# SyncE's order of issue inside an attention slot: the shift ahead of the stacks, and a finished group's rows and denominators loaded in two slots

## The reference

```python
x = queries
q = relu(layernorm(x) @ Wq.T + bq); k = relu(keys @ Wk.T + bk); v = relu(values @ Wv.T + bv)
score = einsum('bhsd,bhtd->bhst', qh, kh) / sqrt(8)
a = einsum('bhst,bhtd->bhsd', softmax(score), vh)
a = transpose(a, (0, 1, 3, 2)).reshape(...)            # per head, feature before token
x = x + layernorm(a + layernorm(x))
x = x + layernorm(ffn(layernorm(x)))                   # self-attention, experts, two layer norms
```

## Time and profile before

| | |
|---|---|
| median of 3 runs | 668.88 us (664.58 to 671.4) |
| the profiled execution | 670.79 us, of which the span of the core is 669.0 us |
| busy in the span | PE 532.2, PEld 212.6, DVE 539.4, ACT 429.6, POOL 229.0 us |
| cross-attention, slots 0 to 31 | from about 70 to 403 us of the span |
| the rest of the program (self-attention, experts) | from 403 us to the end |
| chain that ended last | PE 38%, DVE 27%, POOL 15%, ACT 8%, issue 8%, DMA 3% |

### The profile page before, as it was taken

How to read it: one execution, slowest core, us unless ns; L and a number is a source line. 1 busy time by engine, 2 the same in 40 slices (tenths; PEclk the granted TensorE clock), 3 DMA queues, 4 the chain that set the end, 5 groups by cost and what they waited for, 6 DMA issues and landing times.

```text
span 669.0 us, 9878 instructions
## 1 busy us (share of the span) xinstructions
PE 532.2 (80%) x3439; PEld 212.6 (32%) x3439; DVE 539.4 (81%) x867; ACT 429.6 (64%) x914; POOL 229.0 (34%) x360
## 2 busy tenths in 40 slices
PE   2884799999999998999999988476587685998710
PEld 1550122222222222222222215355467542443300
DVE  4969699999999998999999800988838156899996
ACT  2550489998898888988889885134344404566554
POOL 7001000000034440354403650662344401676761
PEclk9995599999999999999999999688687775999955
DMA  9832010111111111201221002000000000000112
GB/s 243 255 136 106 14 37 23 40 33 46 54 60 30 34 53 47 65 26 32 59 57 49 8 9 62 15 1 1 0 1 1 1 1 0 0 1 0 32 31 63
DMA packets 31285, 28.92 MB, mean 43 GB/s; under 512 B 6132, under 2 KB 23676, under 8 KB 31236
## 3 DMA queue, kind: packets, MB, share of 16 engines
q1 hardware_dynamic: 29204, 27.31, 13.8%
q10 hardware_dynamic: 2032, 0.98, 0.6%
HBM read 19.23 MB, written 8.65 MB: 42 GB/s over the span
## 4 chain that ended last, share of the span: by engine, by line
PE 38%; DVE 27%; POOL 15%; ACT 8%; issue 8%; DMA 3%; SPq 1%; ACTq 0%; DVEq 0%; POOLq 0%
PE ps L1267 11%; PE ps L1262 8%; DVE row_max L1436 8%; PE ps L1235 4%; PE ps L593 3%; DVE space L872 2%; DVE st L241 2%; POOL space L382 2%; POOL space L384 2%; POOL smallp L379 2%; ACT attended L1384 1%; DMA space<-max_turned 1%; PE ps L578 1%; DVE space L863 1%; DVE space L264 1%
## 5 line engine op out<-in xcount | busy, mean ns | idle before, releaser
L1436 DVE TENSOR_REDUCE row_max<-ps 128x2 f32<-128x1024 f32 x256 | 299.7, 1219 | 20.2 <-PE ps L1235 17.3
L1368 ACT ACTIVATE space<-ps 128x512 f32<-128x512 f32 x512 | 271.9, 605 | 45.0 <-PE ps L1262 44.5
L1262 PE MATMUL ps<-space 51*128 51x512 bf16 x512 | 159.5, 388 | 9.6 <-DMA space<-max_turned 5.8
L1267 PE MATMUL ps<-space 128*32 128x512 f32 x1024 | 138.1, 612 | 3.0 <-ACT space L1368 0.7
L1235 PE MATMUL ps<-space 48*128 48x512 bf16 x512 | 128.8, 401 | 14.2 <-DVE row_max L1436 12.5
L1137 POOL CAST max_parts<-row_max 128x16 bf16<-128x16 f32 x32 | 6.3, 197 | 269.9 <-DVE row_max L1436 269.9
L1262 PEld LDWEIGHTS ps<-space 51*128 51x128 bf16 x512 | 41.2, 94 | 170.9 <-ACT space L1368 149.1
L593 PE MATMUL ps<-W,space 128*128 128x512 f32 x128 | 72.0, 646 | 0.0
L428 POOL TENSOR_TENSOR space<-PC,same_row 128x512 f32<-128x512 f32 x32 | 32.8, 1057 | 62.9 <-DVE PC L768 62.9
L710 ACT ACTIVATE space<-ps,weight 128x128 f32<-128x128 f32 x128 | 34.3, 383 | 21.2 <-PE ps L593 9.5
L1235 PEld LDWEIGHTS ps<-space 48*128 48x128 bf16 x512 | 26.6, 94 | 54.9 <-DVE row_max L1436 49.1
(11 more groups left out here) (192 smaller groups left out, 701.0 us busy)
## 6 DMA issues: line engine op xcount, KB each, us to landing
q_parts_dram<-space SPq DMA_DIRECT2D x2, 1536.0 KB, 5.5
space<-q_parts_dram SPq DMA_DIRECT2D x64, 48.0 KB
attended_dram<-attended SPq DMA_DIRECT2D x128, 18.0 KB
X<-in_L_attn_queries SPq DMA_DIRECT2D x8, 256.0 KB, 7.7
space<-in_L_ffn_w SPq DMA_DIRECT2D x2, 1024.0 KB, 5.9
space<-q_parts_dram SPq DMA_DIRECT2D x64, 32.0 KB
space<-attended_dram SPq DMA_DIRECT2D x16, 128.0 KB, 2.4
space<-inverses_dram SPq DMA_DIRECT2D x16, 128.0 KB
```

Of the source, the lines that this page charges most:

```text
L1262: pe.matmul(ps[:, col_bank(v), :], k_rows[rows_a, kappa // 4 % 2, tc * P:(tc + 1) * P], q_stack[rows_a, kappa % 4, b * S:(b + 1) * S], sta ...
L1267: mm = pe.matmul(ps[32 * m:32 * m + 32, PV, :], v_heads[:, tc, PAIR * (kappa // 4) + m % PAIR, :], probs[:, tc % 2, m, :], start=(tc == 0) ...
L1368: act.activation(probs[:, tc % 2, m, :], ps[:, col_bank(v), :], ACT.Exp, scale=1.0 / math.sqrt(DH)).then_inc(s_pr, 1)
L1436: dve.tensor_reduce(row_max[:, par].rearrange("p (a c) -> p a c", a=PAIR)[:, :, item], ring(n), AX.X, MAX).then_inc(s_free, 1)
```

## The change

In a slot, SP now stores `attended`, issues the shift of the next slot, and only then the stack of `kappa + 3` with its keys. Behind these, and no longer ahead of the slot, it loads a finished group's denominators in the slot c = 1, and its attended rows in c = 2, followed there by the store of the inverses. The loads of the inverses stay at the head of c = 3. DVE's inversion moves from the third quarter of its slot c = 1 to the second quarter of c = 2.

```diff
-            def load_attended(g):
+            def await_attended(g):
                 for par in range(2):
                     sp.wait_ge(s_ast[par], 64 * 4 * (g + 1))
+
+            def load_denominators(g):
+                for h in range(NH // G):
+                    den = a_dram[:, g * (NH // G) + h:g * (NH // G) + h + 1, DH:DH + 1, :]
+                    sp.dma_start(den_sb[32 * h:32 * h + 32], den.rearrange("b h o (j f) -> (h o j) b f", f=D)).then_inc(s_dl, 16)
+
+            def load_attended(g):
                 for h in range(NH // G):
                     src = a_dram[:, g * (NH // G) + h:g * (NH // G) + h + 1, 0:DH, :]
                     sp.dma_start(A[32 * h:32 * h + 32, g:g + 1].rearrange("p o b f -> p (o b) f"),
                                  src.rearrange("b o d (j f) -> (o d j) b f", f=D)).then_inc(s_al, 16)
-                    den = a_dram[:, g * (NH // G) + h:g * (NH // G) + h + 1, DH:DH + 1, :]
-                    sp.dma_start(den_sb[32 * h:32 * h + 32], den.rearrange("b h o (j f) -> (h o j) b f", f=D)).then_inc(s_dl, 16)
...
             def slot(kappa):
+                g, c = kappa // 8, kappa % 8
+                if g and c == 3:
+                    load_inverses(g - 1)
+                if kappa:
+                    sp.wait_ge(s_pve, kappa)
+                    store_attended(kappa - 1)
+
+                if kappa + 1 < NQ:
+                    sp.wait_ge(s_pr, turn_item(kappa + 1) + 1)
+                    load_shift(kappa + 1)
+
                 if kappa + 3 < NQ:
                     if kappa:
                         sp.wait_ge(s_sc, column_item(kappa - 1, TC - 1, QB - 1) + 1)
                     load_stack(kappa + 3)
                     if (kappa + 3) % 4 == 0:
                         load_keys((kappa + 3) // 4)
-                if kappa:
-                    sp.wait_ge(s_pve, kappa)
-                    store_attended(kappa - 1)
-
-                if kappa + 1 < NQ:
-                    sp.wait_ge(s_pr, turn_item(kappa + 1) + 1)
-                    load_shift(kappa + 1)
+                if g and c == 1:
+                    await_attended(g - 1)
+                    load_denominators(g - 1)
+                if g and c == 2:
+                    load_attended(g - 1)
+                    store_inverses(g - 1)
 
             for kappa in range(NQ):
-                g, c = kappa // 8, kappa % 8
-                if c == 1 and g:
-                    load_attended(g - 1)
-                if c == 2 and g:
-                    store_inverses(g - 1)
-                if c == 3 and g:
-                    load_inverses(g - 1)
                 slot(kappa)
             sp.wait_ge(s_pve, NQ)
             store_attended(NQ - 1)
+            await_attended(G - 1)
+            load_denominators(G - 1)
             load_attended(G - 1)
...
                 def between(tc):
-                    if g and c == 1 and tc == 2:
+                    if g and c == 2 and tc == 1:
                         dve_invert(dve, g - 1)
```

## The result

The changed kernel takes 715.22 us (median of 5 runs, 706.24 to 718.37) against 668.88 us before (664.58 to 671.4, also 5 runs). The ratio is 1.066, with a 95% interval of 1.060 to 1.071. Ratios leave out the runs that lie more than 1.5% above the fastest run of their kernel (here the one of 718.37 us), medians are of all runs. Forecast were 696.4 us in a range of 682 to 709: the direction and the main mechanism held, the size did not. The profiled execution is the fastest of the five, 706.24 us with a span of 704.5; the forecast for a profiled execution was 698.3.

A forecast was written before the change was run, and what follows sets the result against it. Three engines (DVE, ACT, PE) were taken to bound each 9.94 us slot as a closed loop with next to no slack. Terms 16.8 + 9.8 + 7.2 - 6.3 = 27.5 us gave 696.4 us, range 682 to 709.

The forecast's parts named there:

- 7 slots with keys: Slots where keys load last, behind shift and stack: keys land 8.1 us after the shift's issue, 1.4 us lost each, 9.8 us.
- slot 0's stack: First slot's stack, issued behind the shift: there is room because its rows come late, so no loss.
- regained: Late shifts at group ends and the statistics' delay go into the longer slots: -6.3 us, an upper end.
- The stack behind the shift: Every ordinary slot: stack releases TensorE 7.5 us after the shift's issue, wanted after 6.21; 0.8 us lost, 21 times, 16.8 us.
- The shift itself: SP's queue in ordinary slots: the shift waits for ACT's copy of the turned maxima, so it can't be issued earlier.
- Denominators in c = 1: Four DMAs behind shift, stack and keys end 2.4 us before the next shift is wanted: costed at nothing.
- DVE's statistics: Two stretches of four slots: their 1.9 us delay is hidden in the new, longer slots.
- The tail: After the last slot: inversion earlier by less than 2 us, but DVE waits for TensorE 4.21 us anyway; gains nothing.
- the step of c = 3: Group ends: loads of the inverses wait for their store, next shift and stack 2.4 us late, three times, 7.2 us.
- B: Rival: a stack lands as fast as a shift, releasing TensorE 6.65 us after the shift's issue; 677 us, chance 0.08.
- C: Rival: stalls are hidden by PE's waits and DVE's ring, group ends regain 4.4 us; 664.5 us, chance 0.05.
- D: Rival: nothing of a stall is regained and the statistics are paid too; 16 us more, 712 us, chance 0.1.

The follow-up runs named there:

- E7: Changed kernel with four of the six DMAs of each stack left out from slot 4 on; 671.9 us, ratio 1.004 to the kernel before.
- E3: Changed kernel with the store of the inverses issued ahead of the four loads of attended rows in c = 2; 706.0 us, ratio 1.058.
- E8: Changed kernel with the old slot order and the store of the inverses ahead of the attended rows; 674.1 us, ratio 1.010.
- E6: Changed kernel with ten extra matmuls on TensorE ahead of its wait for the stack in each slot computing rows ahead; 708.1 us, ratio 1.061.
- E5: Kernel before, slot order kept, with a group's denominators loaded at the head of c = 1, attended rows at the head of c = 2; 667.7 us, ratio 1.0005.
- E4: Changed kernel with two of the six DMAs of each stack left out from slot 4 on; 694.7 us, ratio 1.038.
- E1: Kernel before with only the order inside a slot changed, stack and keys behind the shift; 698.9 us, ratio 1.049.
- E9: Kernel before with the new slot order, denominators at the head of c = 1 and attended rows at the head of c = 2; 697.4 us, ratio 1.042.
- E2: Changed kernel with stacks and keys moved back to the old slot order, only the groups' loads and inversion changed; 684.7 us, ratio 1.022.

## Why the prediction was wrong, step by step

The direction, the stack's lateness and the rise of ordinary slots were right. What failed are two terms: the landing of the store in c = 3, and TensorE's clock, which had no term at all. A table by the steps of the sum, over the spacings of the copies of turned maxima in the first profile:

| step | forecast | measured in the first profile |
|---|---|---|
| 18 ordinary slots | 0.8 each, 14.4 | 0.88 each, 15.8 (0.75 in the 16 at full clock) |
| 7 slots with keys | 1.4 each, 9.8 | 1.77 each, 12.4 (1.18 in the 4 at full clock) |
| 3 slots c = 3 | 3.2 each, 9.6 | 6.0 each, 18.1 |
| slot 0's stack | 0 | 0.6 |
| regained | -6.3 | -9.0, of which 2.0 in a slot that had begun at half clock before |
| behind the attention, and the rest | 0 | -2.4 |
| sum | 27.5 | 35.5 |

**Right.** *The stack behind the shift:* released 7.35 us behind the shift's issue against 7.5, and 0.58 us regained against 0.5; the row of slot 0 and the late shift of slot 10 were the right rows to price it with. E7 shows that it is this landing and nothing else in the order, as far as shorter stacks can show it. *The shift itself* goes no earlier in ordinary slots. *Denominators in c = 1* cost nothing: their stores and the next shift were in time. *DVE's statistics* are mostly hidden in the new stalls. *The tail:* DVE waits 6.4 us for TensorE behind its last inversion, so the earlier inversion buys nothing.

**Wrong, the step of c = 3.** The forecast put the shift 2.4 us late; it was 4.2, 4.9 and 3.2. The term took 1.6 us for the landing of the store, from a row in which nothing large stood ahead of it. Behind four DMAs of 128 KB the loads could start 2.6, 3.9 and 3.4 us after the store's issue, together 5 us more than 3 x 1.6. I had said that a whole slot lay between the store and its loads before, and then still used the landing time from there. E3 and E8 show that with the store first the wait is gone. The shifts were 5 us later in all than the forecast's 3 x 2.4, and that is 5 us of the miss.

**Wrong, a term that was missing: the clock.** The prediction read the full granted clock of the kernel before in an ordinary slot and carried it over into a kernel whose TensorE stands still in every slot. Stalls that move the loop by half a microsecond were priced at the full clock on their far side. In the first profile the seven slots that run partly at half clock, or begin in it, are about 10 us longer than their like, by an estimate from the spacings in the table. The other terms of the table came out some 7 us below the forecast together, so that this profile is only 8 us above it. The median lies 9 us above the profile, and the forecast had put it 1.9 below: these 11 us go with the clock, though only by correlation. The profiled execution is the fastest, with a mean clock of 0.882 over the whole program, the slowest has 0.858, and the three profiles order by their mean clock. Which part of the 11 us the half clock makes is not measured. E6, which keeps TensorE busy, points the same way, with 14 us at half clock in its profile. The scatter alone proves nothing: the kernel before, in 17 runs beside E5 and E6, lies between 664.6 and 681.6 us.

*The rivals.* B (a stack lands as fast as a shift, 677 us) is refuted: the release at 7.35 is what the trace of slot 0 said. The rule of the Trainium skill that stood beside it, in "DMA: Bandwidth & Descriptors", section "Anatomy of one DMA", puts the fixed cost at about 2.0 us, told of the GpSimd path; here, on SyncE's queue, the landing took 2.5 us from the issue of the last DMA of a stack, and 3.5 us from that of the fourth of four in E4. C (hidden, 664.5) is refuted by E1 and E9, although its point of decision, 6.7 us, was about right: the slot of E4 with its release at 6.6 us takes 9.93, and those from 6.9 on are longer. D (nothing regained, 712 us) comes nearest to the median, by luck: its mechanism is wrong, since 0.58 us are regained in the ordinary slot above, and the 16 ordinary slots at full clock are 0.75 us longer and not 1.3.

## What to carry to other kernels

Moving a DMA earlier in a queue moves another one later: price the one that gives way, from its new moment of landing to the moment at which it is wanted, before the one that gains. Here a shift that could not go earlier was put ahead of a stack with 6 us to spare, and it needed 7. Where a change makes TensorE stand still once in every round of a loop, give the half clock behind such stalls a term of its own, and take more than one profile before you size it. A small store whose landing is waited for belongs ahead of large loads and not directly ahead of its readers.

## What the runs showed of the hardware

- In the kernels with 23 to 28 stalls of TensorE on stacks, one a slot, of 0.3 to 2.6 us (the changed kernel, E1, E3, E9), its granted clock fell to 0.50 for 3.4 to 17 us at a time, three to seven times in one attention, at places that moved from execution to execution. In the changed kernel's three profiles all 18 falls came with or at most 1.6 us behind an idle time of 1.4 to 3.5 us. With no idle time of more than about 0.9 us in the slots it stayed at 1.00 for 341 us on end (E7). But it also fell with no such idle time before it, in the last two slots (E2 for 30.7 us, E5 for 6.8). Work without use in the stall left 14 us at 0.50 in the one profile of E6, against 31 to 61.
- Leaving out the two smallest of a stack's six DMAs (a sixth of its bytes together) moved its landing by some 0.4 us only, though SP issued for 2.76 us instead of 3.72; data moved for about 4 us in both. Leaving out four (half of the bytes) brought the release from 7.35 to 5.3 us behind the shift's issue, seen in the slots c = 3. The landing here isn't the last issue plus a constant.
- A store of 64 KB that landed 1.6 us after its issue with nothing large ahead of it took 2.6, 3.9 and 3.4 us behind four loads of 128 KB, by the time SP waited.
